# Row-sum reciprocals laid along the rows by transfers through DRAM, in a fused four-layer graph network on one core

## Time and profile before

| | |
|---|---|
| median of the runs | 2619.9 us |
| the profiled execution | 2621.08 us, its span 2619.3 us |
| PE, DVE, ACT, POOL busy | 97%, 75%, 72%, 29% of the span |
| mean granted PE clock | 0.989 |
| instructions | 50145 |
| bytes moved by DMA | 132.14 MB, mean 50 GB/s |
| DMA packets' time | 20.7% of 16 engines' span on the queue that SP feeds |

### The profile page before, as it was taken

The page is one execution under the profiler, slowest core; times in us unless marked ns, Lnnn a source line. Parts: engine busy times, 40 slices in busy tenths (PEclk is TensorE's granted clock), DMA queues, the critical chain, the costliest instruction groups (busy, mean ns, idle before and its releaser), DMA issues.

```text
span 2619.3 us, 50145 instructions
## 1 busy us (share of the span) xinstructions
PE 2544.9 (97%) x17384; PEld 2048.2 (78%) x17384; DVE 1973.5 (75%) x5487; ACT 1896.5 (72%) x4273; POOL 756.2 (29%) x1081
## 2 busy tenths in 40 slices
PE   4999999999999999999999999999999999999997
PEld 3877777887878888787887878888788887778875
DVE  4867867868687786887868788786887868776776
ACT  3767857769587695867769587695877859575787
POOL 1222242322413223142322413224142232323221
PEclk7999999999999999999999999999999999999999
DMA  3312203122031221302122031221212223021122
GB/s 117 73 27 49 52 20 69 32 61 60 26 70 42 53 51 45 73 22 65 38 54 67 21 76 41 53 52 45 66 29 55 48 51 69 19 51 27 31 63 54
DMA packets 91082, 132.14 MB, mean 50 GB/s; under 512 B 15921, under 2 KB 40146, under 8 KB 90834
## 3 DMA queue, kind: packets, MB, share of 16 engines
q1 hardware_dynamic: 90834, 128.94, 20.7%
HBM read 19.83 MB, written 8.39 MB: 11 GB/s over the span
## 4 chain that ended last, share of the span: by engine, by line
PE 91%; DVE 4%; issue 1%; ACT 1%; POOL 1%; SPq 1%; DMA 0%; DVEq 0%; ACTq 0%; POOLq 0%
PE bank L1226 18%; PE bank L1227 17%; PE bank L1228 17%; PE bank L1283 16%; PE bank L1298 9%; PE bank L1275 8%; PE bank L1303 2%; PE bank L1266 2%; PE bank L1336 1%; DVE probs L1031 1%; SPq L624 1%; DVE vh L1097 0%; ACT probs L805 0%; DVE gate L1008 0%; DVE gate L1132 0%
## 5 line engine op out<-in xcount | busy, mean ns | idle before, releaser
L805 ACT ACTIVATE probs<-probs,few 128x512 f32<-128x512 f32 x1024 | 732.5, 720 | 88.8 <-DVE few L1031 84.4
L1031 DVE CUSTOM_DVE_ANT_0 probs<-bank,mask 128x512 f32<-128x512 f32 x1024 | 677.3, 683 | 58.3 <-PE bank L1283 26.3
L1283 PE MATMUL bank<-ident,probs 128*128 128x128 f32 x4096 | 585.4, 273 | 8.9 <-ACT probs L805 7.1
L1283 PEld LDWEIGHTS bank<-ident,probs 128*128 128x128 f32 x4096 | 484.1, 141 | 92.8 <-issue 27.9
L1275 PE MATMUL bank<-stack 96*128 96x512 f32 x1024 | 415.2, 451 | 1.8 <-DMA stack<-qk 0.7
L814 ACT ACTIVATE PT<-bank 128x512 f32<-128x512 f32 x630 | 354.6, 597 | 51.3 <-PE bank L1303 25.8
L1042 DVE COPY PT<-bank 128x512 f32<-128x512 f32 x394 | 269.0, 688 | 84.7 <-PE bank L1283 46.4
L727 POOL TENSOR_TENSOR feat<-o,feat 128x256 fp32r<-128x256 f32 x128 | 95.2, 744 | 615.1 <-ACT feat L827 606.3
L1226 PE MATMUL bank<-feat,W 128*128 128x512 f32 x640 | 259.9, 406 | 0.0
L1298 PE MATMUL bank<-PT,vh 128*32 128x256 f32 x4096 | 254.8, 383 | 1.1 <-issue 0.7
L840 ACT ACTIVATE res<-res,few 128x256 f32<-128x256 f32 x256 | 139.6, 593 | 156.8 <-POOL few L712 155.0
(11 more groups left out here) (110 smaller groups left out, 4995.6 us busy)
## 6 DMA issues: line engine op xcount, KB each, us to landing
stack<-qk SPq DMA_DIRECT2D x768, 128.0 KB, 2.4
res<-in_x_dram SPq DMA_DIRECT2D x16, 512.0 KB, 3.8
out_dram<-res SPq DMA_DIRECT2D x16, 512.0 KB, 2.9
rows<-bo_sum SPq DMA_DIRECT2D x15, 128.0 KB, 2.9
rows<-in_L_gnn_bias_dram SPq DMA_DIRECT2D x14, 128.0 KB, 2.9
rows<-in_L_gnn_ln_beta_dram SPq DMA_DIRECT2D x14, 128.0 KB, 2.9
PT<-in_adj_dram SPq DMA_DIRECT2D x1, 1024.0 KB, 5.4
PT<-in_L_gnn_w_w_dram SPq DMA_DIRECT2D x2, 512.0 KB, 6.7
```

The costliest lines, as they stand in the source:

```text
L805: k = act.activation(p, p, ACT.Exp, bias=least[:, t % P_RING:t % P_RING + 1], scale=-1.0, accum_out=sums[:, grp % 2, q * HG + h:q * HG + h ...
L1031: k = dve.tensor_tensor_reduce(out=probs[:, t % P_RING, :], in0=place("scores", t)[:, :], in1=mask[:, half * QT + q, :], scale=1.0, scalar ...
L1283: k = pe.transpose(place("transpose", t)[:, m * P:(m + 1) * P], probs[:, t % P_RING, m * P:(m + 1) * P], ident[:, :])
```

## The change

The reciprocals no longer pass POOL, PE and ACT. SP issues, when `recip` is done, two transfers (`keep`, one for each query tile) from `sums` to a scratch tensor `recips` in DRAM, laid out as head x query. Each moves 128 x 4 single elements of 4 bytes. When both have landed (and the `o32` of the group before has been read), SP issues one transfer (`spread`) that reads each head's row of 256 elements 32 times into 32 partitions of `o32`. `out1` waits for the values and for that transfer. `rsum`, the two transposes and `out0` are gone. The tables of costs and delays have new entries, so that all lists are placed anew.

```diff
-TILE_US = {..., "recip": 0.12, "rsum": 0.62}
+TILE_US = {..., "recip": 0.12}
-VALUES_US = {1: (1.86,), 2: (0.89, 1.19)}
+VALUES_US = {1: (1.68,), 2: (0.89, 0.89)}
-SP_US = {"row": 0.6, "load": 0.6, "store": 0.6, "stack": 1.9}
+SP_US = {"row": 0.6, "load": 0.6, "store": 0.6, "stack": 1.9, "keep": 0.6, "spread": 0.6}
-LATE = {..., "recip": 0.2, "rsum": 0.2, "values": 0.25, ...}
+LATE = {..., "recip": 0.2, "values": 0.25, ..., "keep": 3.0, "spread": 3.0}
...
-        add("exp", "ACT", ("exp", t), ("stt", t), *([("rsum", grp - 2)] if grp >= 2 else []))
+        add("exp", "ACT", ("exp", t), ("stt", t), *([("keep", grp - 2)] if grp >= 2 else []))
...
-            add("rsum", "POOL", ("rsum", grp), ("recip", grp),
-                *([("pool", "out3", grp - 1)] if grp else []))
+            add("recips", "SP", ("keep", grp), ("recip", grp))
+            add("recips", "SP", ("spread", grp), ("keep", grp), *([("pool", "out3", grp - 1)] if grp else []))
...
-            add("out", "ACT", ("act", "out0", grp), ("values", grp, PARTS - 1))
-            add("out_dve", "DVE", ("dve", "out1", grp), ("act", "out0", grp), frees=[("values", grp)])
+            add("out_dve", "DVE", ("dve", "out1", grp), ("values", grp, PARTS - 1), ("spread", grp), frees=[("values", grp)])
...
+        recips = nc.dram_tensor("recips", [2, HG, QH], F32, kind="Internal").ap()
...
+                elif key[0] == "keep":
+                    grp = key[1]
+                    if grp >= 2:
+                        sp.wait_ge(spread, 16 * (grp - 1))
+                    sp.wait_ge(recip_ready.sem, recip_ready.at(grp))
+                    for q in range(QT):
+                        sp.dma_start(recips[grp % 2, :, q * P:(q + 1) * P].rearrange("h p -> p h"),
+                                     sums[:, grp % 2, q * HG:(q + 1) * HG],
+                                     allow_slow_non_contiguous=True).then_inc(kept, 16)
+                elif key[0] == "spread":
+                    grp = key[1]
+                    sp.wait_ge(kept, 16 * QT * (grp + 1))
+                    if grp:
+                        layer, b, *_ = tile_of((grp - 1) * GROUP)
+                        wait_sig(sp, out_lo[b % STREAMS], f"o{layer}{(grp - 1) % GROUPS}", b)
+                    sp.dma_start(o32[:, :], recips[grp % 2].unsqueeze(1).broadcast_to([HG, HD, QH])).then_inc(spread, 16)
...
             def output(grp):
-                dve.wait_ge(rb_ready.sem, rb_ready.at(grp))
+                wait_full(dve, "values", grp)
+                dve.wait_ge(spread, 16 * (grp + 1))
...
                 if part == PARTS - 1:
-                    pe.wait_ge(rsum_ready.sem, rsum_ready.at(grp))
-                    for q in range(QT):
-                        k = pe.transpose(dst[:, QH + q * P:QH + (q + 1) * P], rsum[:, q, :], ident[:, :])
                     fill(k, "values", grp)
```

More of the change, by code:

```diff
@@ L43, in raised_by @@
         self.next += 1
-TILE_US = {"scores": 0.31, "stt": 0.61, "exp": 0.71, "transpose": 0.36, "recip": 0.12, "rsum": 0.62}
+TILE_US = {"scores": 0.31, "stt": 0.61, "exp": 0.71, "transpose": 0.36, "recip": 0.12}
 PT_US = {"ACT": 0.48, "DVE": 0.61}
-VALUES_US = {1: (1.86,), 2: (0.89, 1.19)}
+VALUES_US = {1: (1.68,), 2: (0.89, 0.89)}
 PE_US = {"ax": 2.8, "a": 2.8, "hT": 0.36, "x1T": 0.36, "x2T": 0.36, "x3T": 0.36}
 ACT_US = {"scale": 0.4, "n0": 0.99, "n1": 0.99, "n2": 0.99, "n3": 0.99, "rows2": 0.95, "q": 0.55, "k": 0.55, "r": 0.61,
-          "zt": 0.61, "c": 0.61, "rh": 0.52, "hf": 0.52, "out0": 0.26, "out2": 0.31}
+          "zt": 0.61, "c": 0.61, "rh": 0.52, "hf": 0.52, "out2": 0.31}
 DVE_US = {"scale": 0.4, "w0": 1.66, "mom_o": 0.93, "norm_o": 2.52, "rows2": 1.14, "h": 2.06, "res2": 1.55, "proj3": 1.55,
@@ L55 @@
 POOL_US = {"scale": 2.35, "beta": 2.35, "bo": 2.35, "out3": 0.7}
-SP_US = {"row": 0.6, "load": 0.6, "store": 0.6, "stack": 1.9}
-LATE = {"scores": 0.13, "stt": 0.11, "exp": 0.25, "transpose": 0.28, "pt": 0.25, "recip": 0.2, "rsum": 0.2, "values": 0.25,
-        "pe": 0.2, "act": 0.14, "dve": 0.2, "pool": 0.15, "row": 2.0, "load": 3.5, "store": 3.0, "stack": 2.4}
+SP_US = {"row": 0.6, "load": 0.6, "store": 0.6, "stack": 1.9, "keep": 0.6, "spread": 0.6}
+LATE = {"scores": 0.13, "stt": 0.11, "exp": 0.25, "transpose": 0.28, "pt": 0.25, "recip": 0.2, "values": 0.25,
+        "pe": 0.2, "act": 0.14, "dve": 0.2, "pool": 0.15, "row": 2.0, "load": 3.5, "store": 3.0, "stack": 2.4, "keep": 3.0, "spread": 3.0}
 def nominal(key):
@@ L360, in adj_resnorm_kernel @@
             add("recip", "DVE", ("recip", grp), ("exp", t))
-            add("rsum", "POOL", ("rsum", grp), ("recip", grp),
-                *([("pool", "out3", grp - 1)] if grp else []))
+            add("recips", "SP", ("keep", grp), ("recip", grp))
+            add("recips", "SP", ("spread", grp), ("keep", grp), *([("pool", "out3", grp - 1)] if grp else []))
             for part in range(PARTS):
-                last = part == PARTS - 1
                 add("values", "PE", ("values", grp, part), *(() if part else tail),
-                    *([("rsum", grp)] if last else []), ("dve", "v", b, layer, NT // 2 - 1),
+                    ("dve", "v", b, layer, NT // 2 - 1),
                     opens=() if part else [("values", grp)])
-            add("out", "ACT", ("act", "out0", grp), ("values", grp, PARTS - 1))
-            add("out_dve", "DVE", ("dve", "out1", grp), ("act", "out0", grp), frees=[("values", grp)])
+            add("out_dve", "DVE", ("dve", "out1", grp), ("values", grp, PARTS - 1), ("spread", grp), frees=[("values", grp)])
             add("out", "ACT", ("act", "out2", grp), ("dve", "out1", grp))
@@ L541, in adj_resnorm_kernel @@
         recip_ready = Signal(sem("recip_ready"), groups)
-        rsum_ready = Signal(sem("rsum_ready"), groups)
-        rb_ready = Signal(sem("rb_ready"), groups)
+        kept = sem("kept")
+        spread = sem("spread")
         o32_ready = Signal(sem("o32_ready"), groups)
@@ L746, in feature_lo @@
                 gru_lo[j].raised_by(i, f"{step}{s}{f}")
[L748 to L757, removed]
             for key in order.by_engine["POOL"]:
-                if key[0] == "rsum":
-                    sums_of(key[1])
-                elif key[1] == "rstd":
+                if key[1] == "rstd":
                     rstds(*key[2:])
@@ L815, in move_pt @@
                 pt_act.raised_by(k, t)
[L817 to L820, removed]
             def output_hi(grp):
```

7 lines of the change are left out of this document (2 added, 5 removed).

## The result

| | before | after |
|---|---|---|
| median (4 runs each) | 2619.6 us | 3184.6 us (3176.2 to 3185.6) |
| ratio, 95% interval | | 1.2152 (1.2138 to 1.2166) |
| profiled execution, its span | 2621.1, 2619.3 us | 3176.2, 3174.4 us |
| mean granted PE clock | 0.989 | 0.928 |

565 us over 128 groups are 4.4 us a group. The forecast was 2598 us within 2584 to 2655; even the rival of late transfers stood at 2700.

A forecast was written before the change was run, and what follows sets the result against it. The prediction took PE to bound the kernel: 2621.1 - 28 (transposes) + 1.3 + 2 (tail, first blocks) + 3 (SP) = 2599.4 us; with the median 1.2 us below the profiled run, 2598 us, range 2584 to 2655.

The forecast's parts named there:

- rival of late transfers: DVE at out1: the transfers come after DVE does, out1 is 2.0 us late, kernel 2700 us; chance 0.22.
- What bounds the kernel: Whole kernel: PE is never waiting except 23 us in fill and tail, so a microsecond off PE is one saved.
- Part 1: PE's list: dropping the two transposes saves 0.22 us a group, 28 us in all, between 0 and 56.
- Its own range, from changes of the lists alone: Whole kernel: spread of the forecast time due to newly placed lists, 2590 to 2608 us.
- Part 2: ACT and POOL: losing 128 copies (49.2 us) and the spreading was costed at nothing, since PE is saturated.
- Part 3: Reciprocals' transfers to out1: 6.1 us, arriving 1.3 us before DVE comes to out1, so the new wait costs nothing.
- The way from the reciprocal to SP: Between the reciprocal's end and SP's first issue: some 0.15 us.
- The whole way: From the reciprocal's end to spread's landing: 6.1 us, within 4.4 to 10.5.
- Part 4: SP's list: 128 x 3 more issues in order of planned time, so only the plan's errors cost, 3 us.
- the issue of `keep` itself holds SP: SP's queue: keep's issue holding SP for several microseconds would make the forecast wrong; no row bounds it.
- Part 5: Fill and tail, where PE waits: the added latency costs 1.3 us at the last group, 2 us at first blocks.
- Four engines: spread's transfer: runs on four DMA engines, lands in 3.8 us instead of 2.9, kernel 2606 us; chance 0.12.

The follow-up runs named there:

- e1: The kernel before without POOL's spreading, the two transposes and ACT's copy, no transfers instead, out1 multiplying by gamma, lists placed anew: 2615.0 us, ratio 0.9981.
- e8: The kernel before with its lists, POOL's spreading and ACT's copy kept, only the two transposes left out: 2593.2 us, ratio 0.9902.
- e4: The kernel after with keep written in the order of sums, 128 pieces of 16 bytes per transfer instead of 512 of 4: 2626.9 us, ratio 1.0028.
- e5: The kernel after with its 1024 four-byte pieces written 64 bytes apart in DRAM, spread reading rows of adj: 2628.5 us.
- e7: The kernel after with the same 1024 four-byte pieces written to SBUF, 8 bytes apart, spread reading rows of adj: 2628.3 us.
- e10: The kernel after with its four-byte pieces written 16 bytes apart in DRAM, spread reading rows of adj: 2632.4 us.
- e2: The kernel after with all transfers, but spread lands in a buffer nobody reads and out1 multiplies by gamma: 3001.7 us, ratio 1.1454.
- e3: The kernel after with only the planner's costs of keep and spread changed to those its trace shows: 3015.3 us, ratio 1.1529.
- e9: The kernel after with keep alone, read by nobody, no spread, out1 multiplying by gamma: 2814.7 us, ratio 1.0742.
- e6: The kernel after with spread reading one row into all 128 partitions, outermost dimension 128 instead of 4: 3210.2 us.

## Why the prediction was wrong

**What bounds the kernel (right, and part of the loss).** PE was the bound, so each stall counts. The reading that only fill and tail had idle time, 23 us, left out the first 131 us, where PE idles 38.5 us more; nothing here hangs on it. But with the stalls the clock fell too: it stood at the lower of its two levels for 2% of the recorded time before and for 14% after. e1 and after run the same 17128 matmuls, in 2513.2 us at a mean granted clock of 0.995 and in 2710.5 us at 0.928. Scaling by the clock gives 2513.2 x 0.995 / 0.928 = 2695 us, nearly all of it. Of the 561 us between their spans 197 are slower matmuls and 364 are idle time. No step of the prediction counted this.

**Part 1, PE's saving (right in size, wrong in what it brings).** 0.22 us a group predicted from two timeline rows, 26.7 us measured where the lists stay (e8). With new lists 5 us remain (e1). "Its own range, from changes of the lists alone" was 2590 to 2608; the lists' effect alone exceeded it. Why the placer does worse with less work is open.

**Part 2, ACT and POOL at nothing.** Borne out: e8 keeps their work and is the fastest kernel here, e1 leaves it out and is slower.

**Part 3, the new way of the reciprocals (the step that failed).** Three terms of the sum were mis-sized, one of them badly:
- `keep`, "1.8 to 6.4, taken 2.9 us": from the first issue to the landing it is 0.6 + 9.65 = 10.2 us. The latency, 2.2 us taken, was read off a 1 KB write in one piece and off loads in four-byte pieces; the far end took 38 ns a piece from loads of 1 KB rows. No row of before had small writes next to each other, and what e4, e5, e7 and e10 single out is just that. Neighbours were outside both ends, so the true value was outside too. That an unseen operation gets its far end from the nearest rows, when those differ in the very property that is new, was the weak place.
- `spread`, "2.9 us": 3.4 where the DMA is free, 4.2 in after.
- The way from the reciprocal to SP, "some 0.15 us": 0.7 us at the median, since SP is often not there yet.
- The whole way, "6.1 us, within 4.4 to 10.5": `spread` has landed 15.2 us after the reciprocal, and `out1` starts at 15.5. (The terms of the lower end add up to 4.5.)

The rival of late transfers had the mechanism and the place, but not the price. Its rate, half of what goes beyond 0.4 us of cover, would make some 490 us of `out1`s that start 8.1 us after the planned 7.4; e2 and e3 put 183 and 169 us on DVE's wait. And even so this is a third of the loss; two thirds came by another way.

**Part 4, "I put 3 us on all of it" (the second failure).** e9 and e2 put roughly 200 and 187 us on it. Two things were missed. SP's list was costed as if only errors of the plan counted; with a `keep` of 10 us every `spread` is such an error, and SP stands 767.7 us. And a slow write was treated as a matter of those who wait for it; e9 shows that it delays the transfers behind it, whose `stack`s PE then waits for. The prediction's own last sentence named "the issue of `keep` itself holds SP" as what would undo it; it was not the issue (0.9 us for two), it was the landing.

**Part 5** (3.3 us for fill and tail) can't be told apart in a loss of this size.

**Engines and small pieces.** Four engines: in after the first of `spread`'s five updates stands for 12 and four follow; in e6 there are 16. That agrees with the Trainium skill (page "DMA: Bandwidth & Descriptors", section "Rules for kernel authors", on the engines, and section "Why a DMA increments its semaphore by 16 and not by 1", by which the sequencer posts the rest itself). The rival put 0.9 us on it where 0.5 is shown; it is a small thing beside `keep`. The same page of the Trainium skill, section "Specifications", says that below 512 bytes the engine reads, modifies and writes. I weighed that against loads of small pieces, which was the wrong row, and took it for the slow end of my own bounds; e5 and e7 show small pieces alone to be cheap. The Trainium skill's section "Rules for kernel authors" on that page also warns against transposing with a plain DMA and a rearranged pattern, with a "19× difference" to the hardware's own transpose. I did not weigh it, and it speaks against `keep`, which is such a transfer. No run here has the hardware's transpose; against e4's ordered write `keep` lands 9.65 / 2.0, 4.8 times as late. It would have deserved a rival.

**Still open.** What in the memory's path makes touching four-byte writes slow (only spacings of 4, 16 and 64 bytes were run), by what the delay passes to transfers behind that touch no DRAM, and what the newly placed lists do worse.

## What to carry to other kernels

A transfer that turns a matrix by its access pattern is judged by the pieces as they lie in DRAM, not by its bytes: make the runs long on chip first (here one DVE transpose of 212 ns), and only then write. Before a transfer is put on a queue that feeds the bound engine, ask what it does to those behind it. A wait on the engine that issues the transfers can hold up everything queued there. And when work goes out of a list that a placer makes, time the removal with the old lists and with the new ones: the difference here, 22 of 27 us, was nearly the whole gain.

## What the runs showed that I had not expected

- A transfer's packets can be through in 2 us and its last report come 6 us later; a page of the profile that counts packets' time (24.3% of the queue's engines after, 25.3% in e5) shows nothing of it. The semaphore updates do.
- 1024 four-byte writes in DRAM: touching 9.65 us, 16 bytes apart 3.1, 64 bytes apart 2.6; to SBUF, 8 bytes apart, 2.0; the same numbers as 256 pieces of 16 bytes 2.0.
- A transfer between two SBUF buffers, issued while such a write was on its way, landed after a median of 6.6 us; without one, 2.4 (e9).
- The stretch 1048 to 1310 us of the kernel after has a mean granted clock of 0.91 of full speed (2.4 GHz) with PE busy for 87% of it; before, 1.00 with PE busy for 261.68 of 262 us.
